# A list-scheduled four-layer transformer: finer planning steps, key projection ahead of the gate projection, and the last attention block kept on chip

## What is computed

```python
x = x + attn0(layernorm(x))      # one head of 64, causal softmax, with biases
x = x + ffn0(layernorm(x))       # one product with an fp8-rounded 256x256 weight, plus bias
x = x + attn1(layernorm(x))      # 16 heads of 16, rotary positions, causal softmax, W_O
x = x + ffn1(layernorm(x))       # the layer below
# ffn1, with x_prev the row before (zeros ahead of the first row):
xr = mu_r*x + (1-mu_r)*x_prev;   xk = mu_k*x + (1-mu_k)*x_prev
r  = sigmoid(xr @ W_r.T);        k  = xk @ W_k.T
out = r * (square(relu(k)) @ W_v.T)
```

## Time and profile before

| | us |
|---|---|
| median of 3 runs | 2519.56 |
| lowest and highest | 2517.97, 2519.94 |
| the profiled execution, its own time | 2517.27 |
| its span | 2514.1 |
| busy in the span: PE, DVE, ACT, POOL | 2320.8, 1985.3, 1512.4, 525.7 |
| mean granted TensorE clock | 0.981 |

### The profile page before, as it was taken

One profiled execution on the slowest core, in us unless ns is written; L12 is line 12 of the kernel. 1 busy time (PEld: TensorE's weight loads), 2 busy tenths in 40 slices (PEclk: granted clock), 3 DMA queues, 4 the chain that ended last, 5 costly groups with the idle time before them and its releaser, 6 DMA issues.

```text
span 2514.1 us, 52353 instructions
## 1 busy us (share of the span) xinstructions
PE 2320.8 (92%) x19371; PEld 1053.0 (42%) x19371; DVE 1985.3 (79%) x4326; ACT 1512.4 (60%) x2753; POOL 525.7 (21%) x526
## 2 busy tenths in 40 slices
PE   8889899999999899998999999999999999999998
PEld 4544333333434335353444534344344434332345
DVE  5778689887787887879787787997788688899932
ACT  2234456575655666676675666657566577677762
POOL 5453210302215012120403303031121400000011
PEclk9899999999999999999999999999999999999999
DMA  2322220120211312021121302112021121110111
GB/s 56 83 72 73 76 58 25 38 59 18 83 34 35 82 43 73 15 79 29 42 65 37 91 19 76 40 35 78 12 76 35 42 70 45 31 42 27 28 37 36
DMA packets 185896, 125.41 MB, mean 50 GB/s; under 512 B 84912, under 2 KB 185392, under 8 KB 185648
## 3 DMA queue, kind: packets, MB, share of 16 engines
q1 hardware_dynamic: 184880, 121.16, 17.4%
q10 hardware_dynamic: 768, 0.92, 0.1%
HBM read 62.20 MB, written 59.24 MB: 48 GB/s over the span
## 4 chain that ended last, share of the span: by engine, by line
PE 55%; DVE 29%; ACT 6%; issue 4%; DMA 2%; SPq 2%; DVEq 1%; POOL 1%; POOLq 0%; ACTq 0%
DVE mx L1543 20%; PE psum L1867 12%; PE psum L1845 6%; PE psum L1812 6%; PE psum L1778 4%; ACT probs L1303 4%; PE psum L1742 3%; PE psum L1887 2%; PE psum L1713 2%; PE psum L1898 2%; PE psum L1651 2%; PE psum L1918 2%; PE psum L1799 2%; PE psum L1906 2%; DVE stats L1402 1%
## 5 line engine op out<-in xcount | busy, mean ns | idle before, releaser
L1303 ACT ACTIVATE probs<-psum 128x512 f32<-128x512 f32 x2176 | 1139.4, 607 | 465.8 <-PE psum L1845 310.2
L1543 DVE TENSOR_REDUCE mx<-psum 128x1 f32<-128x512 f32 (+2 forms) x2304 | 1283.4, 620 | 140.9 <-PE psum L1812 99.5
L1867 PE MATMUL psum<-probs,vs 128*17 128x512 f32 (+3 forms) x5120 | 590.7, 543 | 0.7 <-ACT probs L1303 0.3
L1812 PE MATMUL psum<-kst,qst 48*128 48x512 f16 (+3 forms) x2560 | 439.6, 354 | 71.0 <-DVE mx L1543 37.7
L1845 PE MATMUL psum<-qst,kst 50*128 50x512 f16 (+3 forms) x2560 | 428.7, 353 | 55.7 <-DVE mx L1543 19.5
L1812 PEld LDWEIGHTS psum<-kst,qst 48*128 48x128 f16 x2560 | 134.0, 94 | 397.5 <-DVE mx L1543 154.5
L1845 PEld LDWEIGHTS psum<-qst,kst 50*128 50x128 f16 x2560 | 128.2, 94 | 360.1 <-ACT probs L1303 131.4
L1867 PEld LDWEIGHTS psum<-probs,vs 128*17 128x17 f32 x5120 | 93.1, 96 | 155.5 <-issue 127.6
L1088 POOL TENSOR_SCALAR vare<-mv 128x4 f32<-128x4 f32 x64 | 15.5, 241 | 595.5 <-DVE mv L1405 595.5
L1819 PE MATMUL psum<-maskq,identh 64*128 64x128 bf16 (+1 forms) x2048 | 131.1, 205 | 0.0
L1117 POOL TENSOR_TENSOR sums<-probs 128x512 f32<-128x512 f32 x12 | 15.3, 1272 | 494.3 <-ACT probs L1257 494.3
(11 more groups left out here) (173 smaller groups left out, 2876.2 us busy)
## 6 DMA issues: line engine op xcount, KB each, us to landing
qk_dram<-parts SPq DMA_DIRECT2D x168, 128.0 KB
qst<-qk_dram SPq DMA_DIRECT2D x128, 96.0 KB, 2.3
kst<-qk_dram SPq DMA_DIRECT2D x128, 96.0 KB, 2.3
v_dram<-vst SPq DMA_DIRECT2D x64, 136.0 KB, 4.0
vs<-v_dram SPq DMA_DIRECT2D x64, 136.0 KB, 2.1
xs<-x_in SPq DMA_DIRECT2D x16, 512.0 KB, 3.5
x_dram<-xs SPq DMA_DIRECT2D x16, 512.0 KB, 2.9
att_dram<-ast SPq DMA_DIRECT2D x64, 128.0 KB, 2.0
```

The lines of the kernel that those rows point to most:

```text
L1303: act.activation(dst, src, ACT.Exp, scale=DK1 ** -0.5 / LIFT ** 2).then_inc(S["exp"], 1)
L1543: ins = dve.tensor_reduce(mx1[:, n % 2, 2 * g + odd, tile % TPC, c:c + 1], bank(src, at, at + cols), AX.X, ALU.max)
L1812: ins = pe.matmul(two[odd][:, at:at + cols], qst[rows, qslot, pair, P * (tile % TPC):P * (tile % TPC + 1)], kst[rows, kslot, pair, 0:cols] ...
L1867: ins = pe.matmul(bank(7, off, CH, rows=VW, row=32 * h), vtile[:, h, :], probs[:, HG * (step_no(b, hg, k) % PSTEPS) + h, at:at + CH - off] ...
```

## The change

It has three parts. The planner's stretch becomes 25 (was 40), it tries 16 ways (was 8) and looks to the third stretch's end (was the second's), 75 instead of 80. In the tail, the list has key projection, relu and square ahead of gate projection and tanh, and index 1 of `prod` and `mix` ahead of index 0. The last block's `out` writes into a new buffer `attl`, of the shape of `attc`, in place of `ast`; its `put att` is gone; the last chunk's `load att` brings only the other three groups' columns (192 of 256) into `attl` and waits for the landing of the `load att` before in place of its `turn`; the last `turn` "A" reads `attl` and waits for that `out` as well.

```diff
--- before.py
+++ after.py
@@ -58,6 +58,7 @@
 PAIRS0 = [(q, kp) for q in range(NQ) for kp in range(TPC * (q + 1) // 2)]
 PAIR_AT = {s: n for n, s in enumerate(PAIRS0)}
 CHUNKS = [(b, q) for b in range(B) for q in range(NQ)]
+LAST_CHUNK, LAST_BLOCK = (B - 1, NQ - 1), (B - 1, NHG - 1, NQ - 1)
 
 
 def span(q, kb):
@@ -197,7 +198,7 @@
 
 PATIENCE = 0.25
 
-STRETCH, WAYS, MOVE = 40.0, 8, 10.0
+STRETCH, WAYS, MOVE = 25.0, 16, 10.0
 
 
 HOMES = {"D": (0, 2, 4), "E": (0, 1, 2, 3, 4, 5, 6), "P": (6, 5, 4, 3, 2, 1, 0), "O": (6,), "V": (7,)}
@@ -273,8 +274,8 @@
             for way in range(WAYS):
                 weights = self.weights(at, way)
                 trial = state.copy()
-                self.go(trial, then, number, (at + 2) * STRETCH, weights)
-                rank = (max(trial.free_at["PE"], (at + 2) * STRETCH) - trial.work, way)
+                self.go(trial, then, number, (at + 3) * STRETCH, weights)
+                rank = (max(trial.free_at["PE"], (at + 3) * STRETCH) - trial.work, way)
                 if best is None or rank < best[0]:
                     best = (rank, weights)
             at += 1
@@ -549,7 +550,8 @@
         add("PE", "turnout", me, end + 2, 0.43, ("copy out", me), lat=0.1, claim="P", mode="F")
         add("DVE", "out", me, end + 2, 0.63, ("turnout", me), ("put att", block_before(b, hg, q, 2)),
             free=("turnout", me))
-        add("SP", "put att", me, end + 2, 0.1, ("out", me), lat=3.0)
+        if me != LAST_BLOCK:
+            add("SP", "put att", me, end + 2, 0.1, ("out", me), lat=3.0)
 
 
 def tail_jobs(o, b, q):
@@ -567,11 +569,12 @@
     lent = (0, NQ - 1) if c == (0, 0) else None
     add("SP", "load x2", c, key(), 0.1, ("store x2", c), ("store y", p2),
         *[("put", (0, NQ - 1, bl)) for bl in (2, 3) if c in ((0, 0), (0, 1))], lat=4.0)
-    add("SP", "load att", c, key(), 0.1, *[("put att", (b, hg, q)) for hg in range(NHG)],
-        ("turn", p and ("A", *p)), lat=4.0)
+    add("SP", "load att", c, key(), 0.1, *[("put att", (b, hg, q)) for hg in range(NHG) if (b, hg, q) != LAST_BLOCK],
+        ("turn", ("A", *p) if p and c != LAST_CHUNK else None), ("load att", p if c == LAST_CHUNK else None), lat=4.0)
+    direct = ("out", LAST_BLOCK if c == LAST_CHUNK else None)
 
     def turn(ln, source, *after):
-        add("PE", "turn", (ln, *c), key(), 0.87, source, lat=0.1, claim="D", mode="F")
+        add("PE", "turn", (ln, *c), key(), 0.87, source, direct if ln == "A" else None, lat=0.1, claim="D", mode="F")
         add("ACT", "turned", (ln, *c), key(), 1.05, ("turn", (ln, *c)), *after, free=("turn", (ln, *c)))
 
     def both(ln):
@@ -589,19 +592,19 @@
     add("POOL", "carry", c, key(), 0.2, *[("mix", p and (*p, i)) for i in range(2)],
         *[("prod", p and (*p, i)) for i in range(2)])
     turn(3, ("norm", (3, *c)), ("carry", c))
-    for i in range(2):
+    for i in (1, 0):
         add("ACT", "prod", (*c, i), key(), 1.2, *both(3), ("carry", c),
             *[(("R", "K")[i], p and (*p, n)) for n in range(2)], *[("RT", lent and (*lent, bl)) for bl in range(4)])
         add("DVE", "mix", (*c, i), key(), 1.33, ("prod", (*c, i)), *both(3))
-    for n in range(2):
-        add("PE", "R", (*c, n), key(), 1.71, ("mix", (*c, 0)), lat=0.1, claim="P", mode="F")
-        add("ACT", "gate", (*c, n), key(), 0.5, ("R", (*c, n)), ("addv", p and (*p, n)),
-            lent and (("FFN", lent) if n else ("scores0", (*lent, TPC * NQ // 2 - 1))), free=("R", (*c, n)))
     for n in range(2):
         add("PE", "K", (*c, n), key(), 1.71, ("mix", (*c, 1)), lat=0.1, claim="P", mode="F")
         add("ACT", "relu", (*c, n), key(), 0.5, ("K", (*c, n)), *[("WO1", (*c, m)) for m in range(2)],
             free=("K", (*c, n)))
         add("POOL", "sq", (*c, n), key(), 1.04, ("relu", (*c, n)))
+    for n in range(2):
+        add("PE", "R", (*c, n), key(), 1.71, ("mix", (*c, 0)), lat=0.1, claim="P", mode="F")
+        add("ACT", "gate", (*c, n), key(), 0.5, ("R", (*c, n)), ("addv", p and (*p, n)),
+            lent and (("FFN", lent) if n else ("scores0", (*lent, TPC * NQ // 2 - 1))), free=("R", (*c, n)))
     for n in range(2):
         add("PE", "V", (*c, n), key(), 1.71, ("sq", (*c, 0)), ("sq", (*c, 1)), lat=0.1, claim="P", mode="F")
         add("DVE", "gated", (*c, n), key(), 0.6, ("V", (*c, n)), ("gate", (*c, n)), free=("V", (*c, n)))
@@ -799,6 +802,7 @@
 
         xp = sb("xp", [P, 2, TPC, D], F32)
         attc = sb("attc", [P, TPC, D], F32)
+        attl = sb("attl", [P, TPC, D], F32)
         xn3 = sb("xn3", [P, TPC, D], F32)
         attT = sb("attT", [P, DC, CH], F32)
         x3T = sb("x3T", [P, DC, 1 + CH], F32)
@@ -1006,11 +1010,15 @@
                 elif kind == "load att":
                     b, q = item
                     for hg in range(NHG):
-                        att_put(wt, b, hg, q)
+                        if (b, hg, q) != LAST_BLOCK:
+                            att_put(wt, b, hg, q)
                     old = before(b, q)
-                    if old:
+                    if old and item != LAST_CHUNK:
                         wt.job("turn", ("A", *old))
-                    sp.dma_start(attc[:, :, :], att_dram[b, CH * q:CH * (q + 1), :].rearrange(
+                    if item == LAST_CHUNK:
+                        att_loaded(wt, *old)
+                    into, upto = (attl, HG * DK1 * (NHG - 1)) if item == LAST_CHUNK else (attc, D)
+                    sp.dma_start(into[:, :, 0:upto], att_dram[b, CH * q:CH * (q + 1), 0:upto].rearrange(
                         "(t p) d -> p t d", p=P)).then_inc(S["load att"], 16)
                 elif kind == "load x2":
                     b, q = item
@@ -1583,7 +1591,8 @@
                     wt.job("out", block_before(b, hg, q, 1))
                     ps = home("turnout", item).rearrange("p (t h v) -> p t h v", t=TPC, h=HG)
                     link(dve.reciprocal(rec[:, :, :], ps[:, :, :, DK1]))
-                    dve.tensor_tensor(ast[:, n % 2, :, :].rearrange("p t (h v) -> p t h v", h=HG),
+                    into = attl[:, :, HG * DK1 * hg:HG * DK1 * (hg + 1)] if item == LAST_BLOCK else ast[:, n % 2, :, :]
+                    dve.tensor_tensor(into.rearrange("p t (h v) -> p t h v", h=HG),
                                       ps[:, :, :, 0:DK1], rec[:, :, :].unsqueeze(3).broadcast_to([P, TPC, HG, DK1]),
                                       ALU.mult).then_inc(S["out"], 1)
                 elif kind == "add1":
@@ -1642,6 +1651,9 @@
                     if ln == "A":
                         att_loaded(wt, b, q)
                         src = attc
+                        if (b, q) == LAST_CHUNK:
+                            wt.job("out", LAST_BLOCK)
+                            src = attl
                     else:
                         wt.job("norm", item)
                         src = xn3 if ln == 3 else xns[lane(b, q)]
```

## The result

| | before | after |
|---|---|---|
| median, us | 2519.07 (20 runs) | 2525.85 (20 runs) |
| lowest and highest, us | 2511.10, 2524.12 | 2518.69, 2533.77 |
| profiled span, us | 2514.1 | 2527.6 |
| mean granted TensorE clock in it | 0.981 | 0.974 |

The ratio after to before is 1.0026, 95% interval 1.0017 to 1.0036: the change made the kernel slower by some 7 us. I had forecast 2508.6, in a range of 2496 to 2519, and given 0.10 to slower.

What follows compares the result with a forecast made beforehand. PE was taken as nearly full from 400 to 2400 us, most often held by DVE, with latency bounding the last 56 us. Terms -5.0 + 0 - 6 = -11 gave a median of 2508.6 us, 8-in-10 range 2496 to 2519.

Steps and rivals of the forecast that it cites:

- Part 1: Chunk tails: key projection ahead of gate projection shortens the exposed end; -5.0 us, bounds -3.7 and -5.7.
- The step of 1.87 us per exposed chunk: Tails of chunks (3, 2) and (3, 3): R fills PE's gap between K and V; 2 x 1.87 = 3.7 us gained.
- The -1.3 for chunk (3, 1): Tail woven with the last block's attention: V may start earlier; -1.3 us, bounds 0 and -2.0.
- In all other chunks nothing: Tails beside attention work: the next batch's attention covers a chunk's latency, so key projection first gains nothing.
- Part 2: Last block straight into the chunk's rows: DRAM way of 5.8 us stays hidden by 11.6 us slack; 0 gain.
- Part 3: Finer search, changing the order everywhere, wins back planned idle time; -6 us, bounds -16 and +20.
- a quarter of the windows' spread: Random keys on the same work move PE's busy time per 75 us window by 0.5 us, against some 2 us.
- signs of being wrong: Last chunk's turn waiting for `out`, V-to-V staying at 29 us, or idle before the scores' lines growing over 10 us.
- C: Slower: tighter plan stalls PE before the scores' matmuls where the chip is slower than assumed; +9, 2529 us; chance 0.10.
- A: Search's gain comes back as waits; only the tails' exposed 3.7 to 5 us remain: 2515 us; chance 0.21.
- B: Tails of (3, 1), (3, 2) move forward against the last block; only the last tail follows: some 2495 us; chance 0.14.
- D: Last block's `out` held back, so the direct way pays, up to 5.8 us: 2503 us; chance 0.05.

Runs made afterwards that it cites:

- e1: Kernel before with the key projection first in the last two chunks' tails alone, order otherwise the same: 2513.05 us, ratio 0.9976.
- e5: As e1, plus R and K exchanged in all other tails after planning, in an order otherwise unchanged: 2513.74 us, ratio 0.9986.
- e2: Kernel before with only the last block written straight into the chunk's rows; search and tail list unchanged: 2517.68 us, ratio 1.0001.
- e3: Kernel before with the finer search alone: 2515.69 us, ratio 0.9989.
- e4: Kernel before with the key projection first in all tails, planned by the old search: 2527.92 us, ratio 1.0035.
- e6: Kernel before with only another seed (seed 4) of the planner's random keys: 2542.37 us, ratio 1.0087.
- e9: Changed kernel with one pair of small transfers (a chunk's maxima) moved earlier in SP's order: 2520.49 us, ratio to the kernel before 0.9999.
- e14: Kernel before with another seed (seed 1) and true times for SP's jobs in the planner: 2513.43 us, ratio 0.9990.
- e12: Kernel before with the finer search, key projection first in the last two chunks and true SP times in the planner: 2487.55 us, ratio 0.9879.
- e11: Kernel before with only the planner's times for SP's jobs set as the trace shows them: 2490.00 us, ratio 0.9884.
- e10: Changed kernel with the planner's times for SP's jobs set as the trace shows them: 2508.25 us, ratio to the kernel before 0.9966.
- e13: As e11, with the key projection first in all tails: 2492.36 us, ratio 0.9915.

## Why the prediction was wrong, step by step

**Part 1 was right in mechanism and size.** The step of 1.87 us per exposed chunk was measured in the changed kernel's chain as 1.90 (9.02 - 7.12), and e1 gained what two of them give. The -1.3 for chunk (3, 1) was not tested by itself; e5, which exchanges R and K there too, is no faster than e1. "In all other chunks nothing" holds for the exchange (e5), but not for the keys that the planner works with: changing the order of a list that feeds a search redraws everything.

**Part 2 was right.** Nothing gained (e2); the turn of the last chunk follows V, not `out`. The section of the Trainium skill that stands beside it in the prediction describes DMAs issued by gpsimd, and these are SP's; its 5.5 us and the trace's 5.8 agree all the same, and both are hidden.

**Part 3 is the step that failed**: "I take -6, with bounds of -16 and +20". The kernel lost 7 us although part 1 gives 5 and part 2 nothing, so the new order cost about 12 where I had -6. The reasoning was that a quarter of the windows' spread is what random keys move, and that what the plan gains, the chip gains in good part. The first was too small: the finer search alone shortens the plan by 27 us (e3), not 6. The second was wrong: e3 turns 27 planned us into 3 on the chip, e4 turns 11 into a loss of 9, and e6's seed alone costs 24. The search by itself does not contradict the term (e3: -3, interval -6 to +1). What I put at nothing was that search and keys together draw another order, with waits that the plan does not know. Beside such a spread between orders, a term of -6 had no weight, and the range should have been taken from it: I let 0.10 stand for everything above 2519. What I could have done blind is to hold the planner's durations against the trace for every engine. I did so for the exponential only, where I took 7.05 us for fourteen as 0.504 each, though that row includes the last one's whole duration (0.607): the thirteen steps before it take 6.44, 0.496 each, within 4% of the planner's 0.477. The planner is nearly right there. It is wrong on SP by a factor of three to eight, and SP's rows were in the trace: the earlier trace rows has one DMA at 0.36 us where the plan has 0.1.

**The signs.** Every sign of the forecast came, and none of the signs of being wrong: V to V in 27.1 us, 32.7 us from the last turn to the end, that turn behind V and not `out`, 122.8 us of idle time before the two lines of scores (127 or less wanted), 256 fillers (under 311 wanted). They watched the end and the scores, and no sign looked at waits for transfers or at PE's idle time as a whole.

**The rivals.** C had the right sign (+9 forecast, +7 measured) and the right kind of cause, a plan denser than the chip allows, but the wrong place: idle time before the two lines of scores went from 126.7 to 122.8 us and not up. What grew were waits for transfers queued on SP. A's "what it gains comes back as waits" is what happened to the fillers' 12.6 us, and more. B and D did not occur.

**Settled and open.** Shown: the parts' own costs (e1, e2, e5); that an order drawn anew can move this kernel by more than the change does (e6); that one mis-queued pair of transfers accounts for 5 to 7 us of the changed kernel (e9); that all five orders planned with true SP times are faster than their partners, by 23 us on average, and that the lead arises in the first 400 us. How much of a single pair's 7 to 33 us is the queue and how much the luck of a new draw is not shown: only e9 corrects SP's queue in an order otherwise held fixed, and it corrects one place. The longer latency of the maxima's rows, part of the same edit, was not tested apart either.

Not settled: what makes orders with true times still differ by up to 27 us. Among the runs of one kernel time and mean clock go together (the changed kernel: 0.970 at 2533.8 us, 0.981 at 2519.0), but between orders the clock does not sort them: e14's profile has 0.984 at a median of 2513, e12's 0.983 at 2488. Whether the finer search helps is open as well: -3 us (e3 against before), -2 (the changed kernel against e4), -1 with true times (e12 against e11, though e12 has e1's edit, itself worth -5, besides), but +13 (e10 against e13).

## What to carry to other kernels

Where an order is made by simulating a kernel, check every engine's assumed durations against the trace before refining the search, the queue that issues DMAs too: count the DMAs of a job, times the queue's time for one. A better search on a wrong model only finds orders that exploit the error. And before a change to such a kernel is judged, redraw its order with a few seeds; a difference smaller than their spread says nothing about the change, and a part is tested cleanly only in an order held fixed.

## What I had not expected of the hardware

SP's queue is held about as long by a tiny transfer as by a large one. The 128 KB of one DMA of a store cost 0.57 us in the queue, the 2 KB of one DMA of the maxima's rows 0.63, so four tiny transfers hold it for 2.5 us. The Trainium skill, page "DMA: Bandwidth & Descriptors", section "Issuing engines are not separate DMA queues", calls the time it takes to initiate a DMA "usually small relative to the DMA itself"; here twelve stores held the queue for 7.6 us in front of a transfer that PE waited for, so the measurement decides against relying on that. Page "Perfetto Trace Analysis", section "What "DMA-bound" means", names the issuing sequencer as a bound of its own, and with that the trace agrees for this stretch: SP's queue is busy for 8.8 of the 9.0 us from 126.2 to 135.2.

DVE and POOL disturb each other. Four instructions of a norm on DVE take 1.38 us alone and 5.44 beside POOL's additions in SBUF; the kernel before, timeline of both engines:

```profile
170.90 1.27 POOL L1123 TENSOR_TENSOR sums<-sums,probs 128x512 f32<-128x512 f32 x1
170.96 5.44 DVE L1424 TENSOR_SCALAR xn<-xs,mv,rstd 128x256 f32<-128x256 f32 x4
...
172.24 1.26 POOL L1125 TENSOR_TENSOR sums<-sums,probs 128x512 f32<-128x512 f32 x1
...
173.65 1.26 POOL L1123 TENSOR_TENSOR sums<-sums,probs 128x512 f32<-128x512 f32 x1
...
174.99 1.26 POOL L1125 TENSOR_TENSOR sums<-sums,probs 128x512 f32<-128x512 f32 x1
...
176.54 0.63 PE L1651 MATMUL psum<-ident,xn 128*128 128x128 f32 x4 [3.52 <-DVE xn L1424]
```

The row of DVE merges four instructions; they end at 172.31, 173.66, 175.06 and 176.40, each some 0.15 us behind one of POOL's, and PE loses 3.52 us. The changed kernel has the same at 182 us, with 5.06. The Trainium skill, page "SBUF — State Buffer", section "SBUF: two separate sides", describes the port pair that the two engines share as an exclusive lock, held for the whole instruction by whichever starts first; for DVE it names instructions in a 2-port mode or with two SBUF inputs. The trace agrees with such a lock; the mode of these instructions it does not show. The planner knows nothing of this either, and I did not try to remove it. It is not alike in all orders: the norm's instructions on `xp` (L1424, 64 of them) take 407 ns on average in the kernel before and 560 in e6, the seed that lost 24 us. So it is one candidate for the spread between orders, untested.
